# Expert rows scattered by index from GpSimd's queue, low parts of h made by VectorE, score matmuls in three fp32r terms

## The chip, the cores and the metric

The kernel runs on one core of one Trainium2 chip. The metric is the device time of one execution in microseconds (us). Matmuls run on PE (TensorE), elementwise work on DVE (VectorE), ACT (ScalarE) and POOL (GpSimd); SP (SyncE) issues DMAs. "DVEq", "SPq" and the like are the sequencers of these engines.

## What is computed

Two transformer layers over 4096 tokens (2 x 2048) of 256 channels. What the change touches is the mixture of experts of layer 0 and the pattern attention of layer 1:

```python
# layer 0, experts: 8 experts, 2 per token, C = 1280 rows each
probs = softmax(xf @ Wg); top_vals, top_idx = top_k(probs, 2)
keep = loc < C                                # loc: the token's place in its expert
buf = zeros((E, C + 1, h)).at[e_flat, l_flat].set(xk)
a, g = split(einsum('ech,ehf->ecf', buf[:, :C], W_in))
out_e = einsum('ecf,efh->ech', gelu(a) * g, W_out)
y = (out_pad[e_flat, l_flat].reshape(S, K, h) * gates[..., None]).sum(axis=1)
# x = x + attention(xn) + y ; xn = layernorm(x)
# layer 1: 16 heads against 32 patterns, sparsemax, and 8 + 2 small MLPs over all tokens
A = sparsemax(scale * (query @ Wq + bq) . keys); out = A @ values @ Wo + bo
```

## The kernel before

It is one program of six stages, each a block that all engines leave before the next begins: `latents`, `attention`, `experts`, `mixing`, `layer1`, `finish`. On each engine instructions run in the order in which the code writes them; semaphores tie the engines together, and DMA queues are ordered per engine.

**attention** (16 head pairs n of layer 0). Beside the attention, DVE works out each token's expert and its row `slot` in the buffer `buf` (10240 rows: 8 experts x 1280). POOL blanks `buf` with ten 1 MB writes of zeros (L814), masks the causal blocks (L754), loads rows of `xn` (`fetch`, L737) and writes them into `buf` by index (`dispatch`, L743): 64 indirect DMAs of 128 rows, four one after another at each of 16 places.

**experts**. 40 tiles m of 256 rows, five for each expert, in `Fori` loops over pairs of experts. A tile is turned by PE (L1465), multiplied by `W_in` in four steps f of 12 matmuls (L1474), passed through gelu on ACT (L1523), multiplied into `h` on DVE (L1595), and multiplied by `W_out` (L1484, 24 matmuls). Operands of these matmuls are split into a high and a low fp32r part. The high part of `h` comes from ACT (L1527), its low part from POOL (L1516). PE runs the output matmuls of tile m behind step f = 1 of tile m + 1. ACT copies the result out of PSUM (`keep`, L1532) and stores 256 rows of `expert_out` in their expert's order with one plain DMA (`store`, L1536). In tiles 2, 3 and 4 of an expert ACT and DVE also cut two pieces each of the next expert's weights at f = 2 (L1546, L1586). In the first eight tiles after the first DVE also divides the attention's result by its sums (L1612). ACT waits at the end for all stores.

**mixing**. 16 steps t of 256 tokens. PE projects the attention's output (L1727, L1733, L1738), DVE adds the input (L1812), the first expert's row times its gate (L1817) and the second's (L1824), takes layernorm's statistics (L1832 to L1849) with a square root on ACT between them (L1784), ACT normalises (L1788), PE turns the rows (L1748) and makes layer 1's router logits (L1757), DVE picks the top two four steps behind (L1857 to L1866). The experts' rows come through POOL: four indirect gathers of 128 rows a step from `expert_out` by `slot_get` (L1714), three steps ahead, each step's freed by L1824 of three steps before.

**layer1**. 8 chunks c of 512 tokens. For each chunk ten MLPs i: gate (L2079, with a mask in L2084), up (L2089), down (L2105), with silu on ACT (L2170) and the product on DVE (L2261). Between them PE makes the next chunk's scores at i = 6 to 9: for each of four groups t two fp32 matmuls of 512 columns (L2042, four records in the trace) into the one PSUM tile `pZ`, which DVE empties (`keep_scores`, L2204) before the next group can start. DVE sorts the 32 scores of each head (L2223, L2225: 28 passes) and finds the threshold (L2236 to L2253). ACT copies the score columns out of the normalised rows (L2158) at i = 0 and 1. PE turns the weights and mixes (L2053, L2064) at i = 1 to 4.

**finish**. 16 steps of 256 tokens: output projection, sum with `partial`, store.

## Time and profile before

| | us |
|---|---|
| median of 3 runs | 2150.52 (2140.54 to 2154.29) |
| the profiled execution's own time | 2144.84 |
| its span, first to last instruction | 2143.1 |
| PE busy | 1966.0 (92%) |
| DVE busy | 1531.1 (71%) |
| ACT busy | 1035.6 (48%) |
| POOL busy | 514.3 (24%) |

The stages lie at about 0 to 120 us (latents), to 1063 (attention), to 1442 (experts), to 1570 (mixing), to 2096 (layer1) and to 2143 (finish). A row of the timeline or of a group gives the engine, the line of the kernel, the operation, what it writes and reads by the program's names, and how many instructions stand behind it; the square brackets at its end hold the idle time before it and what ended it ("issue": nothing that the profile shows; "remote": a signal whose sender it can't name at that time).

### The profile page before, as it was taken

To read this page: it belongs to the slowest core of one execution; us is meant where nothing else is said; L and a number is where in the kernel's file an instruction comes from. 1 tells how busy PE (TensorE), PEld (TensorE's weight loads), DVE (VectorE), ACT (ScalarE), POOL (GpSimd) and SP (SyncE) were. 2 spreads that over 40 slices of the span, in tenths; PEclk is the share of its full clock that TensorE was granted. 3 is DMA by queue.
4 is the path that set the end of the run, shared out by engine and by line. 5 is a ranking of instruction groups with operands and counts; after the bars stand their busy time and mean duration, and the time that the engine had idled before them with its cause. 6 is when DMAs were issued, how large, how long until landed. Compare 5 with 4: busy or idle time off the path is not lost. (4 is left out here: it accounts for less than half of the span.)

```text
span 2143.1 us, 35073 instructions
## 1 busy us (share of the span) xinstructions
PE 1966.0 (92%) x11874; PEld 1195.0 (56%) x11874; DVE 1531.1 (71%) x3473; ACT 1035.6 (48%) x2246; POOL 514.3 (24%) x932
## 2 busy tenths in 40 slices
PE   6869999999999999999799999986678999999998
PEld 3333333333333333333299999984556777777776
DVE  7879988888888888888054333325578998889883
ACT  3426677676767777777744444432331122221112
POOL 4554123322222222222233333336400000000000
PEclk9979999999999999999999999998789999999998
DMA  6555111111101111110133222215410000000005
GB/s 206 183 160 200 62 38 58 56 38 40 35 32 38 41 43 43 43 43 11 52 101 100 90 84 88 90 42 163 144 51 12 9 21 20 20 20 20 10 11 162
DMA packets 111781, 143.69 MB, mean 67 GB/s; under 512 B 12153, under 2 KB 96769, under 8 KB 111233
## 3 DMA queue, kind: packets, MB, share of 16 engines
q1 hardware_dynamic: 87248, 98.09, 14.3%
q0 software_dynamic: 10400, 31.47, 4.4%
q10 hardware_dynamic: 13968, 12.06, 1.8%
q8 instruction: 88, 1.44, 0.3%
q14 instruction: 77, 0.62, 0.1%
HBM read 85.10 MB, written 56.10 MB: 66 GB/s over the span
## 5 line engine op out<-in xcount | busy, mean ns | idle before, releaser
L854 ACT ACTIVATE at_wt<-at_B 128x512 f32<-128x512 f32 (+3 forms) x1280 | 607.3, 538 | 257.7 <-PE at_B L953 240.8
L1259 DVE TENSOR_REDUCE at_piece_max<-at_A 128x1 f32<-128x512 f32 x768 | 489.0, 684 | 71.3 <-PE at_A L934 61.8
L971 PE MATMUL at_O<-at_wt,at_v 128*32 128x512 f32 (+3 forms) x2560 | 313.9, 543 | 0.0
L754 POOL TENSOR_SCALAR_AFFINE_SELECT at_wt<-at_wt 128x128 f32<-128x128 f32 x512 | 147.8, 294 | 632.6 <-ACT at_wt L854 623.9
L1256 DVE CUSTOM_DVE_ANT_0 at_junk<-at_A,s_hide 128x128 bf16<-128x128 f32 (+3 forms) x512 | 230.5, 487 | 69.6 <-PE at_A L934 69.0
L1474 PE MATMUL ex_H<-ex_xT,ex_w_in 128*128 128x256 f32 x1920 | 247.8, 286 | 4.0 <-DVE ex_xT L1581 4.0
L1474 PEld LDWEIGHTS ex_H<-ex_xT,ex_w_in 128*128 128x128 f32 x1920 | 237.0, 193 | 4.4 <-DVE ex_w_out L1586 4.4
L1595 DVE TENSOR_TENSOR ex_h<-ex_act_a,ex_H 128x256 f32<-128x256 f32 x160 | 66.8, 417 | 212.7 <-ACT ex_act_a L1523 212.6
L2170 ACT ACTIVATE l_act_g<-l_G 128x512 f32<-128x512 f32 x80 | 47.9, 599 | 305.9 <-PE l_G L2084 241.3
L934 PE MATMUL at_A<-s_k,s_q 96*128 96x512 bf16 (+2 forms) x480 | 165.7, 363 | 22.3 <-PEq L104 9.6
L1516 POOL TENSOR_TENSOR ex_hT<-ex_h,ex_hT 128x256 fp32r<-128x256 f32 x160 | 123.1, 774 | 254.3 <-ACT ex_hT L1527 254.3
L953 PE MATMUL at_B<-s_q,s_k 99*128 99x512 bf16 x480 | 160.4, 352 | 6.9 <-ACT at_wt L854 6.3
L2105 PE MATMUL l_D<-s_down,l_h 128*128 128x256 f32 x640 | 153.8, 383 | 2.0 <-DVE l_h L2261 2.0
L934 PE MATMUL at_A<-s_raw_out,s_raw_in 96*128 96x512 bf16 (+3 forms) x400 | 138.5, 355 | 7.1 <-DVE at_piece_max L1259 2.7
L934 PE MATMUL at_A<-s_first_rows,at_q 96*128 96x512 bf16 (+3 forms) x400 | 137.5, 352 | 7.5 <-DVE at_piece_max L1259 1.8
L953 PE MATMUL at_B<-s_raw_in,s_raw_out 99*128 99x512 bf16 (+3 forms) x400 | 137.0, 349 | 2.1 <-ACT at_wt L854 1.9
L2105 PEld LDWEIGHTS l_D<-s_down,l_h 128*128 128x128 f32 x640 | 120.5, 191 | 32.6 <-issue 13.2
L953 PE MATMUL at_B<-at_q,s_first_rows 99*128 99x512 bf16 (+3 forms) x400 | 136.4, 348 | 1.8 <-ACT at_wt L854 1.4
L2079 PE MATMUL l_G<-l_xp,s_gate_up 128*128 128x512 f32 x480 | 137.5, 421 | 0.0
L2089 PE MATMUL l_U<-l_xp,s_gate_up 128*128 128x512 f32 x480 | 131.4, 409 | 0.0
L2225 DVE TENSOR_TENSOR l_order<-l_order 128x1024 f32<-128x1024 f32 x104 | 127.2, 1223 | 1.9
L2223 DVE TENSOR_TENSOR l_order<-l_order 128x1024 f32<-128x1024 f32 x104 | 126.8, 1219 | 0.0
(275 smaller groups left out, 2798.9 us busy)
## 6 DMA issues: line engine op xcount, KB each, us to landing
buf<-at_room POOLq DMA_DIRECT2D x10, 1024.0 KB, 8.7
s_first_rows<-buf SPq DMA_DIRECT2D x40, 256.0 KB, 2.7
expert_out<-ex_y ACTq DMA_DIRECT2D x40, 256.0 KB, 2.2
s_raw_in<-in_W_in SPq DMA_DIRECT2D x8, 1024.0 KB
q_parts<-parts SPq DMA_DIRECT2D x16, 384.0 KB, 3.5
s_down<-in_x SPq DMA_DIRECT2D x8, 512.0 KB, 4.7
xn<-s_raw_in SPq DMA_DIRECT2D x8, 512.0 KB, 5.4
at_v<-v SPq DMA_DIRECT2D x16, 256.0 KB, 3.0
```

Source lines behind the costliest of these rows:

```text
L754: pool.affine_select(block_, block_, [[1, P]], ALU.is_ge, 0.0, base=0, channel_multiplier=-1).then_inc(hidden, 1)
L854: act.activation(wt[(HP * p + h) % NE_][:, q0:CH], pB_of(p, h, u)[:, q0:CH], ACT.Exp, scale=D ** -0.5).then_inc(wt_ready, 1)
L934: pe.matmul(pA[slot % NA][:, 0:w], q[n % 3][0:STACK, h, i * P:(i + 1) * P], k[n % 3][0:STACK, k0:k0 + w], start=True, stop=True).then_inc( ...
L953: pe.matmul(pB_of(p, h, u)[:, q0:CH], k[n % 3][:, kt * P:(kt + 1) * P], q[n % 3][:, h, j * CH + q0:(j + 1) * CH], start=True, stop=True).t ...
L971: pe.matmul(pO[j % 2][rows, q0:CH], vs[n % 3][:, kt // TPC, kt % TPC, :], wt[(HP * p + h) % NE_][:, q0:CH], start=kt < 2 and not late, sto ...
L1256: ins = dve.tensor_tensor_reduce(junk[(HP * i + h) % 4][:, 0:w], pA[slot % NA][:, 0:w], hide[:, CH - w:CH], 1.0, NEG, ALU.add, ALU.max, ac ...
L1259: ins = dve.tensor_reduce(top, pA[slot % NA][:, 0:w], AX.X, ALU.max)
L1474: ins = pe.matmul(pH[f][:, a, :], w_in[w][wq][:, k, cols], xT[i][xq][:, k, :], start=(n == 0), stop=(n == len(terms) - 1))
L2079: ins = pe.matmul(pG[i % 2][:], s[f"gate_up{b}"][:, e, k, :], xp[c % 2][:, a, k, :], start=(a, b, k) == steps[0], stop=(e >= NX and (a, b, ...
L2089: ins = pe.matmul(pU[i % 2][:], s[f"gate_up{b}"][:, e, EC + k, :], xp[c % 2][:, a, k, :], start=(a, b, k) == steps[0], stop=(a, b, k) == s ...
L2105: ins = pe.matmul(pD[t // 2][:, t % 2, :], h[i % 2][:, t * P:(t + 1) * P], s["down"][:, ORDER[i], :], start=False, stop=(i == MLPS - 1 and ...
L2225: dve.tensor_tensor(dv[:, :, 0:half], low, high_m, ALU.max).then_inc(sort_step, 1)
```

## The change

It has these parts.

1. `buf` gets two more columns: a row carries the number of its token in front and behind it the number of its second expert. POOL writes them (two small copies for each `dispatch`, L757 of the changed kernel), from a new constant `token`. Blank rows carry the number 2^20.
2. In `experts` DVE works out from these columns, for each tile, the row of `expert_out` to which each result belongs (`find_target`, two instructions of 128x2). `expert_out` is now ordered by token (8192 rows: first choices, then second choices). POOL writes the result by index, two indirect DMAs of 128 rows for each tile (78 in `experts`; those of the last tile stand at the head of `mixing`). ACT issues no stores and waits for none.
3. POOL makes no low parts of `h`; DVE makes them (`low`), at f one step behind and at f = 3 both of the last two. The loops of POOL, SP and DVE in `experts` are written out.
4. In `mixing` SP loads the experts' rows with two plain DMAs of 256 KB for each step, three steps ahead, behind a wait for all writes. PE waits for `Wout` alone, and only behind its first turn.
5. Rows of tokens that an expert dropped must be zero: `expert_out` is filled with zeros in eight 1 MB writes from POOL's queue, one at the head of each of the head pairs 6 to 13 in `attention`.
6. The score weights go through DRAM and are split in `mixing` into a high part (ACT, at t = 4) and a low part (DVE, at t = 5), 128x1024 each. In `layer1` ACT copies the score columns as a high part in one instruction of 128x512 for each k, DVE makes their low parts (`score_lows`, one 128x512 instruction at i = 2 and one at i = 3), and PE makes each group's scores of six fp32r matmuls in place of two fp32 ones. `seg` is half as long.
7. `finish` reads its rows from two tiles, since the second half of them now lies in the attention's memory; DVE's loop there is written out.

The core of the diff:

```diff
@@ attention, POOL
             def dispatch(n):
                 pool.wait_ge(xrow_in[n % 2], 32 * (n // 2 + 1))
...
                 for w in range(2):
+                    pool.tensor_copy(xrow[n % 2][w][:, 0:E + 2:E + 1], token[:, 2 * n + w]).then_inc(token_set, 1)
...
+                    if p == 0 and 6 <= n < 6 + NO_ROWS:
+                        pool.dma_start(no_rows[n - 6],
+                                       zeros[:, 1:E + 1].unsqueeze(1).to_broadcast([P, 8, E])).then_inc(buf_blank, 16)
@@ experts
             def rows(m, i):
                 wait(sp, xT_made, m - 1)
+                wait(sp, target_ready, 2 * (m - 1))
                 sp.dma_start(x[i], one(rows_in, m)).then_inc(x_loaded[i], 16)
...
         @block.gpsimd
         def _(pool):
-            with pool.Fori(0, ROUNDS) as j:
-                for i in range(PAIR):
-                    for f in range(FC):
-                        pool.wait_ge(h_high, FC * (PAIR * j + i) + f + 1)
-                        pool.tensor_tensor(hT[i % 2][1][:, f, :], h[i % 2][:, f, :],
-                                           hT[i % 2][0][:, f, :].bitcast(F32), ALU.subtract).then_inc(h_low, 1)
+            def store(m, t):
+                if t == 0:
+                    pool.wait_ge(target_ready, 2 * (m + 1))
+                    pool.wait_ge(y_ready, m + 1)
+                pool.indirect_dma_start(
+                    out=d["expert_out"], out_offset=bass.IndirectOffsetOnAxis(ap=target[m % 8][:, t:t + 1], axis=0),
+                    in_=y[m % 2][:, t, :], in_offset=None, bounds_check=TOPK * NT - 1, oob_is_err=False,
+                ).then_inc(y_stored[m % 2], 16)
...
             def keep(m, i):
                 act.wait_ge(y_made, m + 1)
-                wait(act, y_stored[i], 16 * (m // 2))
+                if isinstance(m, int) and m == LAST:
+                    act.copy(s["last_y"], pY[i][:]).then_inc(y_ready, 1)
+                    return
+                wait(act, y_stored[i], 16 * RT * (m // 2))
                 act.copy(y[i][:], pY[i][:]).then_inc(y_ready, 1)
...
+            def find_target(m, u):
+                dve.wait_ge(x_loaded[u % 2], 16 * (m // 2 + 1))
+                wait(dve, y_stored[u % 2], 16 * RT * (m // 2 - 3))
+                dve.tensor_scalar(second[u][:], x[u % 2][:, :, E + 1], float(m // PER), float(NT), ALU.is_equal,
+                                  ALU.mult).then_inc(target_ready, 1)
...
+            def low(m, b, f):
+                dve.wait_ge(h_high, FC * m + f + 1)
+                dve.tensor_tensor(hT[b][1][:, f, :], h[b][:, f, :], hT[b][0][:, f, :].bitcast(F32),
+                                  ALU.subtract).then_inc(h_low, 1)
@@ mixing, SP, then DVE
+            def load_rows(t):
+                wait(sp, sums, SUMS * (t - NR + 1))
+                for k in range(TOPK):
+                    sp.dma_start(ye[k][t % NR][:], ye_rows[k][t]).then_inc(rows_in[t % NR], 16)
...
             for t in range(NR):
                 load(t)
+            for i in range(2):
+                sp.wait_ge(s["y_stored"][i], 16 * SLOTS // P // 2)
+            for t in range(NR):
+                load_rows(t)
...
+                if t == SPLIT_AT + 1:
+                    dve.wait_ge(aT_ready, SPLIT_AT + 2)
+                    dve.tensor_tensor(s["to_scores1"][:], scores_raw[:], s["to_scores0"][:].bitcast(F32), ALU.subtract)
@@ layer1, PE, ACT, DVE
                 if t == 0:
-                    pe.wait_ge(score_cols, EC * (c + 1))
+                    pe.wait_ge(score_low, EC * (c + 1))
                     wait(pe, wT_ready, TPC * (c - 1))
                 wait(pe, z_ready, TPC * c + t)
-                for k in range(EC):
-                    ins = pe.matmul(pZ[:], xT_score[:, k, t, :], s["to_scores"][:, k, :],
-                                    start=(k == 0), stop=(k == EC - 1))
+                steps = [(a, b, k) for a, b in TERMS for k in range(EC)]
+                for a, b, k in steps:
+                    ins = pe.matmul(pZ[:], xT_score[a][:, k, t, :], s[f"to_scores{b}"][:, k, :],
+                                    start=(a, b, k) == steps[0], stop=(a, b, k) == steps[-1])
                 ins.then_inc(z_made, 1)
...
+            def score_lows(c, k):
+                dve.wait_ge(score_cols, EC * c + k + 1)
+                dve.tensor_tensor(score_view(1, k), score_rows(c, k), score_view(0, k).bitcast(F32),
+                                  ALU.subtract).then_inc(score_low, 1)
```

The order of instructions at three places. DVE in `experts`, from one tile's first product to the next tile's (the tile of the first expert in which the first two pieces of weights are cut; `ex_h` is the product, `ex_xT` the low part of the turned rows, `ex_w_in` the cut weights, `s_attn` the division). Before:

```order
L1595 TENSOR_TENSOR ex_h<-ex_act_a,ex_H 128x256
L1581 TENSOR_TENSOR ex_xT<-ex_XT,ex_xT 128x512
L1595 TENSOR_TENSOR ex_h<-ex_act_a,ex_H 128x256 x2
L1586 TENSOR_TENSOR ex_w_in<-s_raw_in,ex_w_in 128x512 x2
L1595 TENSOR_TENSOR ex_h<-ex_act_a,ex_H 128x256
L1612 TENSOR_TENSOR s_attn<-s_attn,ex_over_sum 128x512 x2
L1595 TENSOR_TENSOR ex_h<-ex_act_a,ex_H 128x256
```

and changed, where `ex_hT` is the low part of `h`:

```order
L1638 TENSOR_TENSOR ex_h<-ex_act_a,ex_H 128x256
L1610 TENSOR_TENSOR ex_xT<-ex_XT,ex_xT 128x512
L1638 TENSOR_TENSOR ex_h<-ex_act_a,ex_H 128x256
L1615 TENSOR_SCALAR ex_second<-s_first_rows 128x2
L1619 TENSOR_TENSOR ex_target<-ex_second,s_first_rows 128x2
L1628 TENSOR_TENSOR ex_hT<-ex_h,ex_hT 128x256
L1638 TENSOR_TENSOR ex_h<-ex_act_a,ex_H 128x256
L1624 TENSOR_TENSOR ex_w_in<-s_raw_in,ex_w_in 128x512 x2
L1628 TENSOR_TENSOR ex_hT<-ex_h,ex_hT 128x256
L1638 TENSOR_TENSOR ex_h<-ex_act_a,ex_H 128x256
L1628 TENSOR_TENSOR ex_hT<-ex_h,ex_hT 128x256 x2
L1661 TENSOR_TENSOR s_attn<-s_attn,ex_over_sum 128x512 x2
```

The low part of step 1 now stands between the cut weights and the product of step 3, and those of steps 2 and 3 stand behind that product; the two target instructions stand behind the product of step 1.

SP's queue at the head of `mixing`, before (`mx_x` the input rows, `x1b` the sum's store):

```order
L1690 DMA mx_w_out<-in_Wout 128x2x256
L1691 DMA mx_lb_bias<-in_lb_bias 128x8
L1695 DMA mx_x<-in_x 128x2x256 x3
L1701 DMA x1b<-mx_x 128x2x256 [waits mx_sums]
L1695 DMA mx_x<-in_x 128x2x256 [waits mx_sums]
```

and changed (`mx_ye` the experts' rows):

```order
L1742 DMA mx_w_out<-in_Wout 128x2x256
L1746 DMA mx_x<-in_x 128x2x256 x3
L1751 DMA mx_ye<-expert_out 128x2x256 [waits y_stored1,y_stored0]
L1751 DMA mx_ye<-expert_out 128x2x256 x5
L1759 DMA mx_lb_bias<-in_lb_bias 128x8
L1760 DMA mx_scores_raw<-scores_raw 128x1024
L1763 DMA x1b<-mx_x 128x2x256 [waits mx_sums]
L1746 DMA mx_x<-in_x 128x2x256 [waits mx_sums]
L1751 DMA mx_ye<-expert_out 128x2x256 [waits mx_sums]
```

Six loads of experts' rows and the wait for both halves of the writes came in behind the first input rows, two more behind each later input load; the router's bias moved behind them. POOL's 64 gathers are gone, and two scatters stand there instead.

PE in `layer1` at i = 6 of a chunk, before:

```order
L2079 MATMUL l_G<-l_xp,s_gate_up 128x512 x6
L2084 MATMUL l_G<-l_unsel,s_neg_ident 128x128 x4
L2089 MATMUL l_U<-l_xp,s_gate_up 128x512 x6
L2042 MATMUL l_Z<-s_to_scores,l_xT_score 128x512 x2
L2105 MATMUL l_D<-s_down,l_h 128x256 x4
```

and changed:

```order
L2153 MATMUL l_G<-l_xp,s_gate_up 128x512 x6
L2158 MATMUL l_G<-l_unsel,s_neg_ident 128x128 x4
L2163 MATMUL l_U<-l_xp,s_gate_up 128x512 x6
L2116 MATMUL l_Z<-s_to_scores,l_xT_score 128x512 x6
L2179 MATMUL l_D<-s_down,l_h 128x256 x4
```

Nothing moved there; the two score matmuls became six.

## Rows read from the trace of the kernel before

**Rows 1.** Page: busy time of each engine in us, share of the span, instructions

```profile
PE 1966.0 (92%) x11874; PEld 1195.0 (56%) x11874; DVE 1531.1 (71%) x3473; ACT 1035.6 (48%) x2246; POOL 514.3 (24%) x932
```

**Rows 2.** Busy time by stretch: attention, experts, mixing; header names the columns

```profile
core 0: us, PE busy (x) PEld busy (x) DVE busy (x) ACT busy (x) POOL busy (x), PEclk, DMA share, GB/s
190.00:1060.00 870.00, 838.63 (x5280) 280.88 (x5272) 699.98 (x1994) 618.15 (x1317) 226.93 (x593) 1.00 0.15 49
1073.00:1441.00 368.00, 364.83 (x3033) 364.15 (x3034) 138.23 (x260) 175.78 (x441) 123.15 (x160) 0.99 0.26 85
1454.00:1570.00 116.00, 74.99 (x391) 64.06 (x389) 69.78 (x336) 38.55 (x80) 54.48 (x58) 0.78 0.44 132
```

**Rows 3.** One tile's instructions in mixing: ns min/median/max, first and last start

```profile
L1812 DVE TENSOR_TENSOR mx_part<-mx_W,mx_x x16: 678/683/692, 1454.9 to 1558.8; 128x512 f32<-128x512 f32 x16
```

**Rows 4.** Timeline of mixing, DVE: start us, us, work, idle before it and releaser

```profile
1454.88 0.69 DVE L1812 TENSOR_TENSOR mx_part<-mx_W,mx_x 128x512 f32<-128x512 f32 x1 [17.84 <-issue]
1455.61 0.92 DVE L1817 SCALAR_TENSOR_TENSOR mx_part<-mx_ye,s_gates,mx_part 128x256 f32<-128x256 f32 x2
...
1461.86 0.68 DVE L1812 TENSOR_TENSOR mx_part<-mx_W,mx_x 128x512 f32<-128x512 f32 x1
...
1522.67 0.68 DVE L1812 TENSOR_TENSOR mx_part<-mx_W,mx_x 128x512 f32<-128x512 f32 x1
...
1527.23 0.68 DVE L1812 TENSOR_TENSOR mx_part<-mx_W,mx_x 128x512 f32<-128x512 f32 x1
```

**Rows 5.** Waits from 1441 to 1595 us: total us, times, longest us

```profile
ACT mx_aT L1779 <- remote: 33.2, 5, 10.4
...
POOL mx_ye L1714 <- issue: 17.1, 56, 0.3
```

**Rows 6.** Timeline of mixing's longest stall, and POOL in an undisturbed step

```profile
1469.58 0.94 POOL L1714 DMA_INDIRECT mx_ye<-expert_out,s_slot_get  x1 [0.30 <-issue]
1473.47 0.59 ACT L1779 COPY mx_aT<-mx_A 128x512 f32<-128x512 f32 x1 [10.40 <-remote]
...
1525.46 0.94 POOL L1714 DMA_INDIRECT mx_ye<-expert_out,s_slot_get  x1 [4.05 <-DVE mx_x L1824]
```

**Rows 7.** All gathers of POOL in mixing, by line: ns min/median/max, first and last start

```profile
L1714 POOL DMA_INDIRECT mx_ye<-expert_out,s_slot_get x64: 940/946/1099, 1445.6 to 1545.9; - x64
```

**Rows 8.** Timeline between experts and mixing: the last store and the first loads

```profile
1442.20 0.38 ACTq L1536 DMA_DIRECT2D expert_out<-ex_y  x1
1444.84 0.37 SPq L1690 DMA_DIRECT2D mx_w_out<-in_Wout  x1
```

**Rows 9.** Timeline of one tile of experts in which weights are cut

```profile
1388.42 0.59 ACT L1532 COPY ex_y<-ex_Y 128x512 f32<-128x512 f32 x1 [2.20 <-PE ex_Y L1484]
...
1391.09 1.41 DVE L1586 TENSOR_TENSOR ex_w_out<-s_raw_out,ex_w_out 128x512 fp32r<-128x512 f32 x2 [0.39 <-ACT ex_w_out L1546]
...
1392.42 0.41 DVE L1595 TENSOR_TENSOR ex_h<-ex_act_a,ex_H 128x256 f32<-128x256 f32 x1
...
1392.87 0.41 ACT L1527 CAST ex_hT<-ex_h 128x256 fp32r<-128x256 f32 x1 [0.71 <-DVE ex_h L1595]
...
1393.35 0.74 POOL L1516 TENSOR_TENSOR ex_hT<-ex_h,ex_hT 128x256 fp32r<-128x256 f32 x1 [0.25 <-ACT ex_hT L1527]
...
1394.41 0.76 PE L1484 MATMUL ex_Y<-ex_w_out,ex_hT 128*128 128x256 f32 x5
```

**Rows 10.** Timeline of attention behind a burst of four scatters

```profile
420.17 0.97 POOL L743 DMA_INDIRECT buf<-at_xrow,s_slot_put  x1 [0.30 <-issue]
...
421.94 0.39 PE L934 MATMUL at_A<-s_first_rows,at_q 96*128 96x512 bf16 x1 [1.09 <-DVE at_piece_max L1259]
```

**Rows 11.** Timeline of layer1 at the score matmuls

```profile
1630.72 3.78 PE L2042 MATMUL l_Z<-s_to_scores,l_xT_score 128*128 128x512 f32 x4 [5.33 <-DVE l_z L2204]
...
1671.19 0.69 DVE L2261 TENSOR_TENSOR l_h<-l_act_g,l_U 128x512 f32<-128x512 f32 x1 [0.53 <-issue]
...
1700.16 1.65 PE L2089 MATMUL l_U<-l_xp,s_gate_up 128*128 128x512 f32 x6
...
1701.65 1.88 PE L2042 MATMUL l_Z<-s_to_scores,l_xT_score 128*128 128x512 f32 x4
```

## What it will do to the time

> **What bounds the kernel now.** I read the page's busy times first: PE has work for 1966.0 of 2143.1 us and no other engine comes near it [rows 1]. The busy times by stretch then say where the rest lies [rows 2]. In attention PE is busy for 838.6 of 870 us, in experts for 364.8 of 368; in mixing for 75.0 of 116 only, and there no engine is full: DVE has 69.8, ACT 38.6, POOL 54.5. So mixing is bound by a chain, and it is the one stage in which much can be won without taking work from PE.
>
> The steps of mixing are measured by L1812, the first DVE instruction of a step. Its 16 starts lie between 1454.88 and 1558.8 [rows 3, 4], so a step takes 103.9 / 15 = 6.93 us on average. Where nothing disturbs it, a step takes 1527.23 - 1522.67 = 4.56 [rows 4]. The average is made by a few stalls. In the table of waits ACT's copy L1779 waits five times for something "remote", 33.2 us in all, 10.4 at the most, and POOL's gathers wait 0.30 us each for nothing that the profile shows: they run back to back [rows 5]. The longest stall ends at 1473.47, when the last gather of a run of them (1469.58 to 1470.52) is 3 us past [rows 6]; PE's signal, for which ACT waits there, reaches it only then. This is what the row shows; that the gathers hold the signal up is my reading of it, since this stall stands where POOL issued without a pause, and in the 4.56 us step POOL had paused for 4.05 ahead of 1525.46 [rows 6]. The 64 gathers of 0.95 us [rows 7] with 0.30 between them are 80 us of POOL's queue.
>
> **The change, part by part.** All of it is reckoned against the profiled execution, 2144.84 us, which stands 5.7 below the median.
>
> *Handover.* Now ACT issues the last store at 1442.20, and SP starts on mixing only at 1444.84, when it has landed [rows 8]; the first use of an expert's row, L1817, stands at 1455.61 [rows 4]. After the change ACT waits for no store: SP can start at about 1442, 2.8 earlier. What comes last is now a different chain: two scatters on POOL (0.95 + 0.30 + 0.95, [rows 7], so until about 1445), their landing, which I take at the 2.64 from the store's issue to SP's start [rows 8] although some of that is the block's own, then two plain loads of about 0.45 each on SP, and as much again for those to land: 1445 + 2.6 + 0.4 + 2.6 = 1450.6. Input rows, `Wout` and PE's first turn, which no longer waits for a load, lie beside it. Gain 5.0; between 2 and 7.
>
> *Steps.* No gathers stand in mixing. The loads of a step are two plain DMAs on SP, behind L1824's signal of two steps before, so they have more than 9 us to land, and SP has nothing else to wait on. Fifteen steps at 4.56 are 68.4. The first step took 6.98 (1454.88 to 1461.86) before any long stall, 2.4 over it [rows 4]; I keep that. The split of the score weights puts one ACT copy and one DVE subtraction of 128x1024 in: the nearest row is 1.41 for two DVE subtractions of 128x512 [rows 9], and I take as much for ACT's and both as on the path: 2.8 (bounds 0 and 2.8, and DVE alone is 60% busy in this stage). 68.4 + 2.4 + 2.8 = 73.6 in place of 103.9: gain 30.3. If only half of the stalls goes, it is 15.
>
> *Experts.* 160 low parts leave POOL (0.74 each, [rows 9]) for DVE, where the product of the same shape takes 0.41 [rows 9]; I take 0.42 (up to 0.74 if DVE should be as slow as POOL at it). DVE is at 138 of 368 us [rows 2] and rises by 67. What matters is the chain into PE's output matmuls. In a tile without cuts the low part made on DVE starts as soon as ACT's high part is there, and is 0.3 shorter than POOL's. In a tile with cuts (three of five, 21 in all) DVE is late: its cut weights end at 1392.50, the low part of step 1 (0.42) now stands ahead of the product of step 3, which moves from 1392.42 to about 1392.85; ACT's high part ends near 1393.7, the low part of step 2 is made in its shadow, and that of step 3 ends near 1394.1. PE starts the output at 1394.41 [rows 9]: 0.3 us of cover is left.
>
> Into this come 78 scatters, two for each tile, right behind ACT's copy of the result. The nearest rows are those of attention, where four scatters stand one after another: the last starts at 420.17, and PE then waits 1.09 us for a result of DVE that had been made in time [rows 10]. For a burst of two I take half, 0.5, less the 0.3 of cover: 0.2 in each of 21 tiles, 4 us in all. The bounds: nothing, where the burst is over before the low parts are due (it starts behind the copy of 1388.42, some 5 us ahead of the output of 1394.41, [rows 9]); and (1.09 - 0.3) x 21 = 17. The wait of ACT's copy for the scatters of two tiles before is covered by two tiles' time (a tile takes some 9 us: 368 us for 40), that of SP for the target rows by the better part of one.
>
> The Trainium skill has a rule that speaks against this part: "SBUF — State Buffer", section "Who interferes with whom", says that a DVE instruction with two SBUF inputs contends with a GpSimd instruction that reads SBUF, over a shared pair of ports that one of them holds for a whole instruction. The low parts are such instructions and the scatters read their indices. The rows bear little of it out: L1817 reads two SBUF operands and takes 0.92 and less for two [rows 4] in the middle of gathers of which the slowest of 64 takes 1.099 against a median of 0.946 [rows 7]. By the rule each tile could lose up to one scatter, 0.97 us [rows 10], before the cover; by the rows nothing. I go by the rows and keep the rule's case among the rivals.
>
> *Layer1.* A group of scores takes 1.88 now, and six fp32r matmuls of the same 512 columns take 1.65 [rows 11]: 0.23 less. Two of the four groups of a chunk wait for DVE anyway; the other two of seven chunks give 7 x 2 x 0.23 = 3.2. In chunk 0 DVE is the bound (PE waits 5.33 for `l_z`, [rows 11]), and two low parts of 0.69 each come in there: 1.4 back. In later chunks they fit into DVE's idle time, of which 0.53 stands ahead of L2261 at 1671.19 [rows 11], nearly a whole one. Gain 2, between a loss of 4 (where every chunk pays a third of its two low parts) and a gain of 6.
>
> *Attention, finish.* 32 small copies on POOL, eight writes of zeros. POOL is busy for 227 of 870 us [rows 2], and its work is not what PE waits for. The scatters there stay as they are. 0, up to 3 lost.
>
> **Sum.** 2144.84 - 5.0 - 30.3 + 4 - 2 = 2111.5; with the 5.7 between this execution and the median, 2117.
>
> **The rivals.**
> - *Forecast:* the stalls are the gathers' and go; about 2117, by its own bounds 2103 to 2129. Chance 0.60.
> - *The stalls stay in part.* The remote waits might be due to the transfers or to something in PE's and ACT's own chain; for this speaks that the gathers' instruction times don't differ where the stall is. With half of them left the gain of the steps is 15: 2132. Chance 0.13, with full stalls (2147) 0.03 of it.
> - *The stalls move into experts.* The gathers' 64 become 80 scatters. If each of the 21 tiles loses 1 us, and the rest of the tiles some 0.2, the loss is 24 in place of 4: 2137. Chance 0.12. (By the rule of the Trainium skill named above, "SBUF — State Buffer", "Who interferes with whom", it would be of this size: up to 0.97 - 0.3 in each of 39 tiles, an estimated 26.)
> - *Slower.* Every tile's low parts or ACT's signals wait for both scatters: 0.97 + 0.30 + 0.97 = 2.24 less 0.3 of cover, 1.94 x 39 = 76 us in place of 4: 2117 + 72 = 2189. The place is the wait of PE ahead of L1484 in each tile; it decides for slower from (37.3 + 21.5) / 39 = 1.5 us a tile on. For it speaks that ACT waited up to 10.4 for a signal beside POOL's queue; against it that only long runs of gathers did this, and that the burst here is 2.2 us long and starts 5 us ahead of its output. Chance 0.08.
> - *More gain.* Experts loses nothing, ACT's split is hidden, handover gives 7, layer1 6: 2105 and below. Chance 0.07.
>
> **Numbers.** A difference of 1% (21.5 us) is about what a measurement can tell from none here. Below 2129 lie the forecast, the last case and a small part of the second: 0.70. Above 2172 lies nearly all of the slower case: 0.07. Between: 0.23. The range of eight in ten reaches from 2100 over both middle rivals to 2141.
>
> **What would show it.** Right: L1812's starts 4.6 apart throughout, no "remote" wait above 1 us in mixing, the first L1817 about 8 us behind ACT's last copy, in experts PE's wait ahead of the output matmuls under 0.3 us on average and PE still at 99%. Wrong: steps above 5.5 us with POOL silent (then the stalls were not the gathers'), idle time of PE in experts named after the low part or ACT, DVE's low parts longer than 0.5 us beside a scatter, a wait of SP's row loads for the scatters that ends after 1450, or a group of scores slower than 1.65.

## The result, and the profile after

| | before | changed |
|---|---|---|
| median, us (5 runs each) | 2149.55 (2140.54 to 2154.29) | 2095.38 (2094.27 to 2099.51) |
| ratio, 95% interval | | 0.9756 (0.9733 to 0.9778) |
| profiled execution's own time | 2144.84 | 2094.65 |
| its span | 2143.1 | 2092.9 |
| PE busy | 1966.0 (92%) | 1938.7 (93%) |

The change makes the kernel 2.4% faster, 54 us between the medians. Forecast were 33 (2150.5 to 2117), and the median lies below the range. The page of the changed kernel has these busy times:

```profile
PE 1938.7 (93%) x11938; PEld 1195.5 (57%) x11938; DVE 1603.4 (77%) x3728; ACT 1031.9 (49%) x2199; POOL 425.0 (20%) x830
```

The stages one by one, on the spans of the two profiled executions. The table's columns are differences between starts of named instructions in the two traces.

| stretch | before | changed | difference | forecast |
|---|---|---|---|---|
| attention, first to last `at_A` matmul | 903.0 | 899.7 | -3.3 | 0 |
| from there to the first matmul of experts | 47.4 | 42.8 | -4.6 | 0 |
| experts, to the last output matmul | 372.4 | 373.6 | +1.2 | +4 |
| to the first step of mixing | 13.6 | 10.0 | -3.6 | -5.0 |
| mixing, first to last step | 104.0 | 70.5 | -33.5 | -30.3 |
| to the first gate matmul of layer1 | 25.5 | 24.6 | -0.9 | (in layer1) |
| layer1, first to last gate matmul | 491.0 | 489.0 | -2.0 | -2 |
| the rest, to the end | 67.8 | 64.4 | -3.4 | 0 |

They sum to -50.1, the difference of the spans (50.2). The other 4 us of the 54 lie between the median and the profiled execution: 4.7 before, 0.7 after. The forecast had kept an offset of 5.7 for both. A row of this table is a difference between two single executions. In five traces that share the changed kernel's attention, on chips where before takes about 2150, that stretch lasted 899.7 to 907.0 us (before: 903.0 and 909.4), and the last row's 64.4 to 68.3 (before: 67.8 twice). So the rows of -3.3 and -3.4 are no larger than what executions of one kernel differ by.

Busy times by stretch, after, to be held against [rows 2]: attention, experts, mixing.

```profile
core 0: us, PE busy (x) PEld busy (x) DVE busy (x) ACT busy (x) POOL busy (x), PEclk, DMA share, GB/s
190.00:1055.00 865.00, 834.36 (x5256) 279.38 (x5255) 698.07 (x1985) 615.82 (x1312) 235.67 (x627) 1.00 0.19 59
1065.00:1434.00 369.00, 366.25 (x3032) 366.07 (x3033) 197.35 (x500) 175.70 (x441) 81.10 (x78) 0.99 0.26 81
1444.00:1526.00 82.00, 64.70 (x389) 55.65 (x387) 70.03 (x337) 39.64 (x81) 0.00 (x0) 0.92 0.63 203
```

DVE has nearly as much work in mixing as before (70.0 us), but in 82 us: it is now the fullest engine there. The steps, answering to [rows 3], and the two waits of DVE at the stage's head:

```profile
L1874 DVE TENSOR_TENSOR mx_part<-mx_W,mx_x x16: 680/683/692, 1444.5 to 1514.9; 128x512 f32<-128x512 f32 x16
...
  PE mx_W L1797: 14.4, 1
  DMA mx_ye<-expert_out: 1.4, 1
```

Fifteen steps in 70.5 are 4.70 each. The first took 5.9, the one with the split 5.7, and the other thirteen 4.4 or 4.6. In the table of waits of the stage no engine waits for "remote" any more; what ACT's copy still waits for is PE, 12.0 in five waits, of which 7.7 is the first:

```profile
ACT mx_aT L1838 <- PE mx_A L1786: 12.0, 5, 7.7
```

The handover, as the timeline of the changed kernel has it:

```profile
1434.84 0.59 ACT L1566 COPY s_attn<-ex_Y 128x512 f32<-128x512 f32 x1 [5.23 <-PE ex_Y L1512]
1435.80 0.37 SPq L1742 DMA_DIRECT2D mx_w_out<-in_Wout  x1
...
1436.51 0.97 POOL L1773 DMA_INDIRECT expert_out<-s_attn,s_slot_put  x1 [7.39 <-POOLq L1371]
1437.79 0.98 POOL L1773 DMA_INDIRECT expert_out<-s_attn,s_slot_put  x1 [0.30 <-issue]
1440.59 0.61 PE L1792 MATMUL mx_W<-s_bias_rows,s_ones_bf 128*128 128x512 bf16 x1 [4.12 <-DMA mx_w_out<-in_Wout]
...
1442.96 2.94 SPq L1751 DMA_DIRECT2D mx_ye<-expert_out  x6
...
1446.51 0.88 DVE L1879 SCALAR_TENSOR_TENSOR mx_part<-mx_ye,s_gates,mx_part 128x256 f32<-128x256 f32 x2 [1.36 <-DMA mx_ye<-expert_out]
```

SP starts 0.4 us behind the last copy instead of 2.7 [rows 8]. The two scatters need 4.2 us from the second one's end to the signal that frees SP's row loads, where 2.6 had been taken. PE waits 4.1 us for the load of `Wout`, which the prediction had beside the path; with it the first step starts at 1444.46, and the wait for the experts' rows adds 1.4 behind that.

The 0.4 is the best case. POOL drains at the end of `experts` too, and right behind its last scatter: the trace has this drain at 8.39 us, ending at 1435.56, 0.13 behind ACT's last copy. In ten of the thirteen traces of the changed kernel and its variants it ends 1.6 us behind that copy and SP starts 1.9 behind it, so there the drain ends the stage, and most of what ACT's missing store wait gives is gone again. In the same ten traces experts took 371.0 to 371.9 us, less than the 373.6 of this one.

### The profile page after: what moved, and what is told of

The parts are those of the page before. It is cut to its first block and busy times, and to the rows that moved or that the text cites. A ratio compares the mean times of both kernels' runs of the same rounds, so it can differ in the third digit from the quotient of the medians.

```text
span 2092.9 us, 35015 instructions
## 1 busy us (share of the span) xinstructions
PE 1938.7 (93%) x11938; PEld 1195.5 (57%) x11938; DVE 1603.4 (77%) x3728; ACT 1031.9 (49%) x2199; POOL 425.0 (20%) x830
## 5 line engine op out<-in xcount | busy, mean ns | idle before, releaser
L1544 POOL DMA_INDIRECT expert_out<-ex_y,ex_target x78 | 81.1, 1040 | 290.5 <-ACT ex_y L1569 271.9
L2299 DVE TENSOR_TENSOR l_order<-l_order 128x1024 f32<-128x1024 f32 x104 | 127.1, 1222 | 1.9
L961 PEld LDWEIGHTS at_A<-s_k,s_q 96*128 96x128 bf16 x480 | 46.9, 98 | 140.2 <-DVE at_piece_max L1284 67.9
## 6 DMA issues: line engine op xcount, KB each, us to landing
buf<-at_room POOLq DMA_DIRECT2D x10, 1032.0 KB, 12.8
```

Source lines behind the costliest of these rows:

```text
L961: pe.matmul(pA[slot % NA][:, 0:w], q[n % 3][0:STACK, h, i * P:(i + 1) * P], k[n % 3][0:STACK, k0:k0 + w], start=True, stop=True).then_inc( ...
L2299: dve.tensor_tensor(dv[:, :, 0:half], low, high_m, ALU.max).then_inc(sort_step, 1)
```

## The experiments

The experiments ran in four groups, each on a chip of its own, beside runs of the kernel before. Before had these medians: 2157.66 in the first group, 2098.59 in the second, 2098.51 in the third, 2151.17 in the fourth. That spread of 2.8% turned out to be the main finding, and times are compared within a group unless another is named.

**Before, with plain loads in mixing.** POOL's block of mixing is gone, and SP has:

```diff
+            def load_rows(t):
+                wait(sp, sums, SUMS * (t - NR + 1))
+                for k in range(TOPK):
+                    sp.dma_start(ye[k][t % NR][:], ye_rows[k][t]).then_inc(rows_in[t % NR], 16)
```

> The kernel before, with one edit in mixing: the 64 gathers of POOL are replaced by 32 plain loads of 256 KB from SP's queue, three steps ahead; POOL does nothing in the stage. The rows loaded are the first 8192 of expert_out in its old order, so they are not the tokens' own. Gathers cause the stalls: L1812's steps fall from 6.93 to 4.4 to 4.6, no remote wait, 30 to 36 us off the time (about 2115 where before is 2150). Rival, the stalls come from the transfers or from ACT's and PE's chain: steps stay above 5.5 and under 15 us are won.

This kernel adds the wrong tokens' rows, so it serves for its time alone. Measured: 2116.31 against 2157.66, 0.9805 (0.9784 to 0.9827), 41 us less. Steps of mixing:

```profile
L1809 DVE TENSOR_TENSOR mx_part<-mx_W,mx_x x16: 682/684/691, 1460.4 to 1529.8; 128x512 f32<-128x512 f32 x16
```

69.4 us for 15 steps, 4.63 each, and no remote wait. This one edit has four fifths of the whole change's gain.

**The changed kernel, with gathers in mixing.**

```diff
-                for k in range(TOPK):
-                    sp.dma_start(ye[k][t % NR][:], ye_rows[k][t]).then_inc(rows_in[t % NR], 16)
...
+            for t in range(STEPS):
+                wait(pool, sums, SUMS * (t - NR + 1))
+                for k in range(TOPK):
+                    for w in range(2):
+                        c = k * TILES + 2 * t + w
+                        pool.indirect_dma_start(
+                            out=ye[k][t % NR][:, w, :], out_offset=None, in_=d["expert_out"],
+                            in_offset=bass.IndirectOffsetOnAxis(ap=row_at[:, c:c + 1], axis=0),
+                        ).then_inc(rows_in[t % NR], 16)
```

> The changed kernel, with one edit in mixing: SP's plain loads of the experts' rows are replaced by 64 indirect gathers of 128 rows on POOL by a list of consecutive row numbers, three steps ahead. The result and the rows read are the same, in the same order of addresses. Gathers on POOL cause the stalls: steps of L1874 return from 4.69 to 6 to 7 and the time is 25 to 40 us over the changed kernel's (2120 to 2135 on a scale where that is 2095). Rival, it was the scattered addresses of before: within 5 us of the changed kernel.

Measured: 2151.34 against 2157.66, 0.9975 (0.9954 to 0.9996). Against the 0.9756 of the changed kernel in its own comparison that is some 47 us lost, more than the 25 to 40 expected. The first row below is of its steps (114.0 us), the second of its waits:

```profile
L1878 DVE TENSOR_TENSOR mx_part<-mx_W,mx_x x16: 683/684/693, 1452.7 to 1566.7; 128x512 f32<-128x512 f32 x16
...
ACT mx_aT L1842 <- remote: 31.6, 6, 9.5
```

The stalls of [rows 5] are back, with consecutive addresses. So on this chip POOL's gathers make them, not the scattered rows.

**The changed kernel, with the low parts of h on POOL.**

```diff
+            for m in range(LAST + 1):
+                for f in range(FC):
+                    low(m, f)
+                    if f == 0 and m:
+                        for t in range(RT):
+                            store(m - 1, t)
```

> The changed kernel with one part undone: POOL makes the low parts of h again, with the two scatters of tile m - 1 behind the low part of step 0 of tile m; DVE makes none. Theory (POOL cannot do both): a scatter pair holds POOL for 2.3 us, the low part of step 1 is late by up to that but is caught up by step 3; what costs is that signals are held during the burst, as before: 0 to 10 us over the changed kernel. Rival (moving the low parts to DVE is what keeps experts at 99% of PE): each tile's output matmuls wait 1 us or more, 40 us and more over.

Measured: 2119.85, 0.9819 (0.9803 to 0.9835): some 14 us more than the 0.9756 would give there. Experts takes 389.9 us in place of 373.6. The waits of PE in the stage:

```profile
PE ex_Y L1512 <- POOL ex_hT L1551: 10.3, 25, 3.0
```

Neither theory's size is met: more than 10, far less than 40. POOL can't carry both without loss: the stage is 0.4 us a tile longer, not 1. The named waits are 10.3 of the 16.3 us, 7.3 of them in 24 tiles and 3.0 in the last; for the rest the trace names nothing.

**The changed kernel, without the writes of zeros.**

```diff
-                    if p == 0 and 6 <= n < 6 + NO_ROWS:
-                        pool.dma_start(no_rows[n - 6],
-                                       zeros[:, 1:E + 1].unsqueeze(1).to_broadcast([P, 8, E])).then_inc(buf_blank, 16)
...
-            pool.wait_ge(buf_blank, 16 * (BLANKS + NO_ROWS))
```

> The changed kernel without the eight 1 MB writes of zeros in attention and the wait for them at its end (rows of dropped tokens keep what stood in memory). The prediction took them at 0: within 2 us of the changed kernel. Rival, they or the wait for them change the end of attention, where the changed kernel was 4.6 us shorter than the one before (POOL's drain at the block's end took 3.18 us there and 7.77 before): then the drain goes back to 7 to 8 us and the time is 4 to 5 us longer.

Measured: 2107.4, 0.9767 (0.9751 to 0.9783), which can't be told from the changed kernel, nor from one 4.6 us slower. But the profile shows the rival's case: the stretch from the last `at_A` matmul to experts is 48.1 us, not 42.8, and PE's first matmul of experts waits as it did before the change. Before, then this kernel:

```profile
1068.82 1.09 PE L1465 MATMUL ex_XT<-s_ident,s_first_rows 128*128 128x128 f32 x4 [5.69 <-PEq L475]
```

```profile
1072.48 1.08 PE L1489 MATMUL ex_XT<-s_ident,s_first_rows 128*128 128x128 f32 x4 [5.70 <-PEq L476]
```

Behind "PEq" stands the end of the block: the trace has a drain of POOL there, which lasts 7.77 us in this kernel and in the one before, and 3.18 in the changed one. It begins when POOL's last mask is made and holds all engines.

**Which of the two shortens the drain.** Two versions of the kernel before, one with the wait alone, one with the writes too:

```diff
             for i in range(2):
                 pool.wait_ge(put[i], 16 * 2 * TOPK * (HPAIRS // 2))
+            pool.wait_ge(buf_blank, 16 * BLANKS)
```

> The kernel before with one line more: POOL waits at the end of attention for its ten blank writes, which are long done. If the wait is what shortens POOL's drain at the block's end, it falls from 7.77 to 3.18 us. If the late writes do it, it stays at 7.77.

> The kernel before with eight 1 MB writes of zeros from POOL's queue at the head pairs 6 to 13 (into rows that are written again later) and the wait for them. If plain writes behind most of the indirect ones shorten POOL's drain, it falls to 3.18 us and the stretch from the last score matmul to the first matmul of experts from 47.4 to about 43; if it is something else of the change, both stay.

Measured, one execution each: 2098.48 for the wait alone, 2093.70 with the writes; before had 2098.59 (2096.85 to 2099.85) in that group. The first matmul of experts, with the wait and then with the writes:

```profile
1050.82 1.09 PE L1466 MATMUL ex_XT<-s_ident,s_first_rows 128*128 128x128 f32 x4 [5.70 <-PEq L475]
```

```profile
1045.59 0.63 PE L1471 MATMUL ex_XT<-s_ident,s_first_rows 128*128 128x128 f32 x4 [1.12 <-PEq L475]
```

The drain is 7.75 and 3.17 us. In all eighteen traces of this study it is 7.75 to 7.78 without the writes of zeros and 3.17 to 3.18 with them. That the writes shorten it is shown, by taking them out of one kernel and putting them into the other; why they do is not.

**The changed kernel again, and the split on POOL.** The second has:

```diff
-                if t == SPLIT_AT + 1:
-                    dve.wait_ge(aT_ready, SPLIT_AT + 2)
-                    dve.tensor_tensor(s["to_scores1"][:], scores_raw[:], s["to_scores0"][:].bitcast(F32), ALU.subtract)
...
+            pool.wait_ge(aT_ready, SPLIT_AT + 2)
+            pool.tensor_tensor(s["to_scores1"][:], scores_raw[:], s["to_scores0"][:].bitcast(F32), ALU.subtract)
```

> The changed kernel itself, once more, as the measure for what runs beside it. 0.9756 of the kernel before; POOL's drain at the end of attention 3.18 us as in its first profile, where the three kernels without the writes of zeros had 7.77 to 7.78.

> The changed kernel with the low part of the score weights (128x1024) made by POOL instead of DVE in mixing. POOL is idle there and DVE is the fullest engine of the stage: mixing 1.2 us shorter, about 0.05% of the time. Rival: the one instruction was hidden, no change; or POOL's work is late for the block's end: 1 to 3 us longer.

Measured: 2087.97, 0.9943 (0.9926 to 0.9959), and 2087.18, 0.9941 (0.9924 to 0.9958). The split's place makes no difference to the time: mixing's steps have 70.9 us with it on DVE and 71.7 on POOL, where 1.2 less was expected. But the first ratio missed what was expected of it by 1.9%, because the kernel before took 2098.59 in this group. In the trace of before with the wait alone, which differs from before in nothing that acts on mixing, the same 64 gathers stand in steps of 4.88 us:

```profile
L1813 DVE TENSOR_TENSOR mx_part<-mx_W,mx_x x16: 681/683/692, 1437.9 to 1511.1; 128x512 f32<-128x512 f32 x16
```

73.2 us in place of 104.0, and no remote wait. In attention too, what PE gets done in a given time differs by chip more than by kernel. Each of the next four rows is of 300 to 1000 us. Before in the first comparison, then before with the wait on this chip:

```profile
300.00:1000.00 700.00, 677.87 (x4281) 230.27 (x4273) 582.24 (x1599) 494.15 (x1052) 190.13 (x488) 1.00 0.13 43
```

```profile
300.00:1000.00 700.00, 689.44 (x4387) 235.71 (x4383) 594.64 (x1632) 505.98 (x1080) 193.98 (x500) 1.00 0.13 43
```

Then the changed kernel in the first comparison, and on this chip:

```profile
300.00:1000.00 700.00, 679.89 (x4304) 230.91 (x4302) 585.52 (x1606) 497.28 (x1058) 201.42 (x527) 1.00 0.17 55
```

```profile
300.00:1000.00 700.00, 689.60 (x4388) 236.14 (x4378) 595.47 (x1636) 505.98 (x1076) 201.13 (x528) 1.00 0.17 55
```

PE gets through 10 to 12 us more of its work in the same 700 us here.

The traces also record updates of semaphores. Of before's 9753 instructions of PE, DVE and ACT that signal, 309 in the first comparison have no record at their semaphore within 1 us behind their end, each of them within 2 us of an indirect DMA of POOL; on this chip it is 4. The first trace has some 400 fewer such records in all, so part of the 309 is a missing record and not a late signal. That signals were late is told by the engines: PE made the turn below from 1461.85 to 1462.45, and ACT, idle since 1463.07, took it up at 1473.47 [rows 6]. The gathers themselves are alike: median 0.946 and 0.948 us, pitch 1.25. So in these traces other engines' signals are held up beside indirect DMAs on some chips and not on others. I write "holding" and "calm" chip below; that it is the chip, and not what else ran near it, is not shown.

```profile
1461.85 0.60 PE L1727 MATMUL mx_A<-s_ident,s_attn 128*128 128x128 f32 x4
```

**Half the gathers, and plain loads from POOL.** Both are made from the version with all gathers. In the first POOL gathers for `k = 0` alone and SP loads the rest:

```diff
-                for k in range(TOPK):
+                for k in range(1):
...
+                sp.dma_start(ye[1][t % NR][:], ye_rows[1][t]).then_inc(x_in[t % NR], 16)
```

In the second POOL issues plain loads:

```diff
-                    for w in range(2):
-                        c = k * TILES + 2 * t + w
-                        pool.indirect_dma_start(
...
+                    pool.dma_start(ye[k][t % NR][:], ye_rows[k][t]).then_inc(rows_in[t % NR], 16)
```

> The changed kernel; in mixing the first expert's rows come by POOL's gathers (two of 128 rows a step, by a list of consecutive numbers) and the second's by a plain load from SP. Where a chip holds signals up beside POOL's indirect DMAs (before's mixing took 104 us on the first chip): POOL issues for 2.5 us of each step and pauses for 2, so if only unbroken runs of gathers hold signals, steps are 4.7 and the time is within 5 us of the changed kernel; if each gather does, half of the 44 us that all the gathers cost there, so 15 to 25 us over. Where a chip holds none (before at about 2099): no difference.

> The changed kernel; in mixing the experts' rows are loaded by two plain DMAs of 256 KB a step, but issued by POOL. On a chip that holds signals: if it is the indirect form or the number of POOL's issues that holds them, steps stay at 4.7 (within 5 us of the changed kernel); if every software DMA does, they grow to 6 and more. On the other kind of chip: no difference.

Both fell on a calm chip (before 2098.51), so the question for holding chips is not answered. Measured: 2095.51, 0.9988 (0.9977 to 0.9999), and 2095.35, 0.9988 (0.9979 to 0.9998). The steps are 73.9 and 74.3 us, 3 over those of SP's loads (70.8 in the fp32 kernel below, on the same chip), though POOL's issues take only 2.5 us of a step or less. With half the gathers all of it is in the first step (9.4 in place of 6.3) and the other fourteen are the same; with plain loads 1.6 is in the first step (7.9), and five of the others take 4.9 in place of 4.6. The changed kernel itself did not run in this group, so what these two are over its 0.9943 of the second can't be laid to the edits; attention alone took 3.3 us more with POOL's plain loads (893.9) than in the second group (890.6).

**Before, with the low parts of h on DVE.**

```diff
-                        pool.wait_ge(h_high, FC * (PAIR * j + i) + f + 1)
-                        pool.tensor_tensor(hT[i % 2][1][:, f, :], h[i % 2][:, f, :],
...
+                        if f:
+                            low(m, b, f - 1)
+                        if f == FC - 1:
+                            low(m, b, f)
```

> The kernel before with one part of the change alone: DVE makes the low parts of h in POOL's place, ACT still stores. The prediction's cover of 0.3 us in cut tiles says: experts within 1 us of before's 372.4 to 373.3, no change of the time. Rival: DVE, 30% to 56% busy, is late for ACT or PE in cut tiles: 0.4 us or more in 21 tiles, 8 us and more.

Measured: 2096.62, 0.9995 (0.9985 to 1.0004). Experts takes 371.5 us where before with the wait had 373.2. The move is free.

**fp32 scores in the changed kernel.**

```diff
-                for a, b, k in steps:
-                    ins = pe.matmul(pZ[:], xT_score[a][:, k, t, :], s[f"to_scores{b}"][:, k, :],
...
+                for k in range(EC):
+                    ins = pe.matmul(pZ[:], xT_score[0][:, k, t, :].bitcast(F32), s["to_scores0"][:, k, :].bitcast(F32),
```

> The changed kernel with the score matmuls as two fp32 ones again, of the high parts alone (the low parts are still made, and not used). The prediction's two layer1 terms: PE 0.23 slower in each of 32 groups, half of them on the path, so the stretch from the first gate matmul to the last grows by 3 to 4 from 489.3 us, and the time by as much. Rival: PE waits for DVE in all of them, 0 to 1 us.

Measured: 2095.37, 0.9988 (0.9978 to 0.9997); the stretch from the first gate matmul to the last is 495.0 us, 5.5 over the 489.5 of the changed kernel on a calm chip. So the six fp32r matmuls are worth 5.5 us in layer1, more than the 3.2 forecast. A group of scores takes 1.56 or 1.66 us where two fp32 ones take 1.88 or 1.98: 0.32 less, not 0.23. Some 4.1 goes back: this kernel, which still makes the low parts, has 495.0, and before with the wait 490.9. The low parts on DVE are the likely reason, but ACT's copies and `seg` differ between these two as well, and were not tried apart.

**Attention on a calm chip.** There the changed kernel loses: 890.6 to 893.9 us against 883.6 to 885.5 with before's attention. PE's waits at 229 us, changed kernel, calm chip:

```profile
229.47 0.23 PE L961 MATMUL at_A<-s_first_rows,at_q 96*128 96x128 bf16 x1 [0.90 <-DMA at_v<-v]
...
232.16 0.61 PE L980 MATMUL at_B<-s_raw_in,s_raw_out 99*128 99x512 bf16 x1 [2.47 <-DMA s_raw_in<-at_max_rows]
```

Two rows of the pages bear on it, changed and before: issued at the same places, the blank writes of the wider buffer take half as long again to land.

```profile
buf<-at_room POOLq DMA_DIRECT2D x10, 1032.0 KB, 12.8
```

```profile
buf<-at_room POOLq DMA_DIRECT2D x10, 1024.0 KB, 8.7
```

The last group had the changed kernel, it with the scores' store moved, and with the blanks spread as well:

```diff
-                if n == 0:
+                if n == 4:
                     sp.wait_ge(act_step, at_act["to_scores1"])
...
-                    if n == 0 and p % 4 == 0:
-                        pool.dma_start(blanks[p // 4], zeros.unsqueeze(1).to_broadcast([P, 8, E + 2])).then_inc(buf_blank, 16)
+                    if n < 2 and p % 8 == 0:
+                        pool.dma_start(blanks[5 * n + p // 8], zeros.unsqueeze(1).to_broadcast([P, 8, E + 2])).then_inc(buf_blank, 16)
```

> The changed kernel, as the measure for the three beside it: 0.976 of the kernel before where that takes about 2150, 0.994 where it takes about 2099.

> The changed kernel with the store of the score weights (SP's queue, attention) at head pair 4 instead of 0, where it stands ahead of the maximum rows on which PE waits 2.5 us at 229. If this store makes the wait: attention 3 to 5 us shorter and the time as much. If the queue is full of blank writes anyway: within 1 us, and the wait stays.

> As the kernel beside it with the store at pair 4, and the ten blank writes of buf spread over head pairs 0 and 1 (every eighth place) instead of pair 0 (every fourth). If the wider blank rows (12.8 us to landing, 8.7 before) hold SP's loads and maximum rows up: attention 5 to 7 us shorter than in the changed kernel, no DMA wait of PE above 1 us from 180 to 240 us. Otherwise no change from the kernel beside it.

> The changed kernel with POOL's gathers in mixing, a second time. On a chip where the kernel before takes about 2150: 40 to 50 us over the changed kernel, mixing's steps 114 us in all. Where it takes about 2099: 5 to 10 us over (POOL's pace of 4 x 1.25 us a step and a later start), steps 75 us in all.

It fell on a holding chip. Measured: 2101.37, 0.9786 (0.9759 to 0.9813); 2101.73, 0.9770 (0.9741 to 0.9800); 2099.03, 0.9764 (0.9736 to 0.9792); 2143.59, 0.9980 (0.9958 to 1.0001). With the store moved alone the wait for `at_max_rows` stays at 2.5 us and attention at 905.3 (904.6 unmoved). With the blanks spread no DMA wait of PE is left from 170 to 245 us, and attention takes 898.3. So it is the blank writes. It is their crowding as much as their width: issued at half the rate, the wide rows land faster than the narrow ones did at the old places.

```profile
buf<-at_room POOLq DMA_DIRECT2D x10, 1032.0 KB, 7.3
```

Of these 6 us only 2 appear in the medians, and the intervals overlap: attention started 2.0 later in that trace, and experts had 373.6 against 371.6, while handover and mixing had 79.4 where the changed kernel had 80.7. It is no clear improvement on a holding chip. On a calm one, where nothing else hides it, it was not run.

The gathers again cost 42 us (2143.59 against 2101.37), their steps 113.3 us, with this wait:

```profile
ACT mx_aT L1842 <- remote: 36.9, 5, 11.7
```

## Why the prediction was right and wrong

**Right.** Mixing bound by a chain with stalls, and the stalls the gathers': two experiments in opposite directions show it, and the undisturbed step read from two starts (4.56) is the step that came (4.4 or 4.6, and 4.70 on average with the first step and the split). Handover and steps together were forecast at 35.3 and came to 37.1. The split was taken at 2.8, all of it on the path; the one step that has it is 1.1 longer than its neighbours. The handover's 3.6 for 5.0 hides two misses, the scatters' landing (4.2 for 2.6) and the drain, which is named nowhere in the prediction. The sign of layer1 held too, but 2.0 for 2 is luck: it is a difference of two terms that were both too small (5.5 for 3.2, and 4.1 back for 1.4).

**Wrong: "Attention, finish ... 0, up to 3 lost".** This is the step that failed, and 7.9 us of the miss stand here. The prediction said that POOL's "work is not what PE waits for", by POOL's busy share. But at the end of the block every engine waits for POOL's drain, and the row that would have shown it stood in the trace of before: the first matmul of experts waits 5.69 us for "PEq L475". The eight writes of zeros, costed at nothing, shorten this by 4.6. No row of before could show that they would, but that row shows that the length of a drain counts. The other 3.3 are not shown to be the change's. They are a balance, which I read from the starts of ACT's 1280 `at_wt` instructions in both first traces, set against each other: 3.0 lost near 229 us to the wider blank writes, 4.2 won in steps of about 1 us at one place of a head pair, beside the bursts of scatters, and 2.1 in the first 60 us, where executions of one kernel differ by as much. Against a calm chip before falls back by 1.1 to 1.9 at most such places and the changed kernel by 1.0. The plain-loads kernel of the first group, which has before's attention, against the gathers kernel beside it gives the same sign: some 3 lost near 226 us, some 10 won at the bursts. What in the bursts differs (the two small copies ahead of them, the later start) was not tried.

**Wrong: the size of experts.** The step "for a burst of two I take half, 0.5, less the 0.3 of cover: 0.2 in each of 21 tiles" failed. It gave 4 us; measured are 1.2 here and none in the ten traces named above (371.0 to 371.9 against before's 372.4). In 40 tiles PE waits for a low part once, in the last, as it waited 2.3 us there before the change:

```profile
PE ex_H L1502 <- DVE ex_xT L1610: 4.4, 1, 4.4
PE ex_Y L1512 <- DVE ex_hT L1628: 1.8, 1, 1.8
```

The low parts took 0.418 as assumed. The contention that the prediction had kept as a rival did show, but on the other side. The scatters of experts, then one of them and the low part over its end:

```profile
L1544 POOL DMA_INDIRECT expert_out<-ex_y,ex_target x78: 972/974/1404, 1082.7 to 1428.2; - x78
...
1183.81 1.40 POOL L1544 DMA_INDIRECT expert_out<-ex_y,ex_target  x1 [0.30 <-issue]
...
1184.88 0.42 DVE L1628 TENSOR_TENSOR ex_hT<-ex_h,ex_hT 128x256 fp32r<-128x256 f32 x1
```

Twelve of 78 scatters last 1.40 us, 0.43 more than the rest, and in each of the twelve a low part of 0.42 begins 1.07 us after the scatter does. Another 36 have a low part that begins earlier in them and last 0.97. All twelve are the second scatter of a tile in which weights are cut, and ahead of the low part one of DVE's weight subtractions (0.68 us) runs from 0.47 us into the scatter on. So where DVE's instructions stand just so, POOL's scatter lasts longer, and it is POOL that pays, off the path. Which of the two subtractions does it was not tried: the low part begins 0.1 us after a scatter is usually over. The Trainium skill ("SBUF — State Buffer", "Who interferes with whom") says that a DVE instruction with two SBUF inputs contends with a GpSimd instruction that reads SBUF, and calls the shared pair an exclusive lock. The twelve long scatters agree with that; the 36 that have a low part in them and last no longer show nothing of it. The price for DVE that was worked out from it, up to a scatter in each tile, was not seen: none of the 160 low parts took more than 0.428.

**Wrong: the offset.** "The 5.7 between this execution and the median" was added to the changed time, where 0.7 was measured. Such an offset says where one execution happened to fall. Before's five runs spread over 13.8 us and the changed kernel's over 5.2, which looks as if the spread were the stalls'; but with the score store moved the changed kernel spread over 12.8, and with all the gathers back, in the first group, over 6.1. So that is not shown. The offset is 5 of the 22 us of the miss (2117 against 2095.4); attention and its end are 7.9, experts 2.8, handover and steps 1.8, and layer1 and the end 4.3.

Of these 22 an experiment shows the 4.6 of the drain. The offset, 3.3 of attention and 3.4 of the end are as large as what executions of one kernel differ by. In the fourth group, on a holding chip again, the same change gave 0.9786, which on 2150.5 would be 2104.5 and inside the range: that the first measurement fell below it is in part luck.

**Not forecastable from one trace.** 3 us of the end are the clock: at before's last score turns and mixes of layer1 the granted clock was 0.61 (three of four turns in 1.06 us, 0.60 after). But it is one execution's: the changed kernel's own last row is 68.0 us in another trace, as long as before's. And the whole size is the chip's: on a calm chip the same change is worth 0.6%, 11 us. There the sum over the stages of two traces (changed against before with the wait) is: drain 4.6, attention -7.0, experts 2.1, handover 2.2, steps 2.3, to layer1 0.9, layer1 1.4, the rest 0.9, together 7.4 of the 8.0 between the spans; the medians differ by 10.6. Of the rivals "the stalls stay in part" (2132) comes nearest to that case in kind, for a reason that it did not name: not that something else makes them, but that they aren't always there.

## What to carry to other kernels

Where another engine's short wait has "remote" or nothing as its releaser while GpSimd issues indirect DMAs back to back, price the indirect DMAs by the whole stall beside them, not by their 0.95 us: 64 of them cost 35 to 47 us here on one kind of chip and 2 to 4 on the other. Look at the ends of blocks as at any other wait: "PEq" ahead of the first instruction of a stage names a drain that no busy share shows; putting indirect DMAs last in a stage can put such a drain there. And don't carry the offset between one execution and the median over to the new time.

## What the runs showed of the hardware

- Beside indirect DMAs of GpSimd, signals between the compute engines arrive late (ACT's longest "remote" wait was 11.7 us), in the first comparison and in the first and fourth group (before at 2150 to 2158 us, mixing's steps at 104 to 114 us with 64 gathers), and not in the second and third (2099 us, 73 to 75 us). Whether it is the chip or what else went on around it is open.
- A drain of GpSimd at a block's end lasts 7.75 to 7.78 or 3.17 to 3.18 us, some 27 us behind its last indirect DMA, according to whether eight plain writes of 1 MB were issued between the indirect ones. Right behind the last scatter of experts it lasted 8.4 and mostly ended the stage, 1.6 us behind ACT's last copy.
- Writes of zeros of 1 MB, issued at the same places, land in 8.7 us with rows of 1024 bytes and in 12.8 with rows of 1032 (medians of ten); issued at half that rate those of 1032 land in 7.3.
- With plain loads of 256 KB issued by GpSimd 15 steps took 74.3 us, with the same loads issued by SP 70.8, on one calm chip and in one trace each; 1.6 of it is in the first step, which differs by more between traces of SP's loads (5.9 to 8.5).
- Of 78 scatters of 0.97 us twelve last 1.40, each beside two DVE subtractions with two SBUF inputs, the second beginning 1.07 us into it; 36 with such a subtraction beginning 0.35 to 0.94 us into them do not last longer.
